# A transformer stack on one core: order of loads, of the first attention, of the norms and of the last sequences, all outside the long loop

## The chip, the cores and the metric

The kernel runs on one core of a Trainium2 chip. The metric is the device time of one execution in microseconds (us). Engines are named as in the profile: PE (TensorE, matmuls), PEld (its weight loads), DVE (VectorE), ACT (ScalarE), POOL (GpSimd), SP (SyncE, which issues the loads and stores).

## The reference

Eight sequences of 256 rows and 128 features pass through one modulated attention, and then through six layers, each a windowed attention with 16 heads of 64 and a gated feed-forward of 341 hidden features. Everything is float32.

```python
x = L0_attn_emb                                            # (8, 256, 128)
mod = (_silu(L0_c) @ L0_wmod).reshape(8, 6, 1, -1)
sa, ca, ga, sb, cb, gb = (mod[:, k] for k in range(6))
ga = (2 * (ga >= 0) - 1) * jnp.maximum(jnp.abs(ga), 0.25)  # gb alike
h = _layernorm(x, axis=-1) * (1 + ca) + sa
x = x + ga * attn(h, W1, W2, W3, Wo)
h = _layernorm(x, axis=-1) * (1 + cb) + sb
x = x + gb * stack(h)

def attn(emb, ...):       # 8 groups of 16 features, softmax over all 256 keys
    q, k, v = (einsum('bse,pe->bsp', emb, W).reshape(B, H, S, D) for W in (W1, W2, W3))
    scores = einsum('bhqd,bhkd->bhqk', _rope(q), _rope(k)) / sqrt(H)
    out = einsum('bhqk,bhkd->bhqd', softmax(scores), v)
    ...                   # and a product with Wo

def stack(x):
    for i in range(6):
        x = attn_layer(shift_tokens(x), ...) + x   # q, k normed and turned by rope, windows of 32, look back by one
        x = ffn_layer(shift_tokens(x), ...) + x    # layernorm, W1, a * gelu(gate), W2
    return x
```

## The kernel before

The program is written engine by engine, each with its own list of instructions in a fixed order; semaphores hold an engine until another has counted far enough. No scheduler moves anything. `CREDIT` (8) is added to many semaphores at the start so that waits of the first passes are already met.

**Start.** SP issues all loads in one row: the constants (`cst`, 640 KB), x (`x1`, 1024 KB, features on the partitions), `cT`, `wmod`, the weights of the first attention, and the first layer's `wqkv`. ACT and DVE form silu of `cT`; PE multiplies it with `wmod` (L527), ACT copies the result to `mod`. Then PE takes the mean over features of each of four chunks of 512 rows (`ln_tensor`, L225) by a product with a constant matrix; DVE subtracts it (L233), ACT squares, PE takes the variance (L228), ACT takes Ln (L247) and Exp (L249) for the inverse root, DVE multiplies (L238) and scales by the modulation (L1249, one instruction for each of eight sequences). POOL sets memory to constants (`memset`) and then splits `wqkv` of the first layer in a high and a low part (`split_weights`, L426: `wqkv_lo` is `wqkv_sb` minus `wqkv_hi`, which ACT has rounded) and forms two rope tables (L417). PE projects V (L542), then Q and K (L551), DVE applies the rope (L1258) and a constant product sums the pairs (L560).

**First attention.** 16 steps `i`, the middle twelve in a loop of two steps a pass. A step holds 8 blocks of 128 queries by 256 keys, in two halves. PE: `a_scores` (L572) of the next step, `a_turn` (L582), which turns a half of P from banks 4 and 5, `a_turn_o` (L603) and `a_attend` (L594), the product with V. DVE: `a_maximum` (L1276, and L1280, the negation), `a_normalise`, `a_stage` (copies of Q and K of the step after next to a fixed place, L1267, L1270), `a_copy_o`. ACT: `a_exps` (L969, 8 a step), `a_copy_p` (L975, two a step: turned P from banks 4 and 5 to `a_pt`, one buffer that lies in `h1`), and `a_stage_v` (L981, V of the next step to a fixed place).

**Second norm.** PE multiplies with Wo for all eight sequences (L632), DVE adds the residual eight times (L1323), then the same norm runs (`ln_tensor`, `ln_vector`, `ln_scalar`) and DVE scales into `h0` (L1333, `modulate`).

**Slots.** 48 slots follow, one for each layer and sequence. In slot `g` two halves of 128 rows go through projection of the next sequence (L671, L674, L675), scores (L724, L731), the product with V (L766), turns in 64-row halves (`turn`, L684), projection out of the sequence before (L788), and the feed-forward of sequence `g` - 3 (`LAG`): up (L806 to L808), gelu, down (L834). Slots 0, 1 and 2 are written out, slots 3 to 46 are a loop on PE and DVE, slot 47 is written out again. SP loads the next layer's weights on the way.

**End.** After slot 47 the feed-forwards of sequences 45, 46 and 47 are left. They use the same banks (7, 1 and 0), so `last_down` does them one after the other; each has two loads of ACT's table, and `final` adds to x. Four stores of 256 KB write the output.

## Time and profile before

| | us |
|---|---|
| three timed runs | 1780.46, 1783.48, 1783.80 |
| the profiled execution | 1771.68 |
| its span, first to last instruction | 1769.9 |
| PE busy in the span | 1633.4 (92%) |
| DVE, ACT, POOL busy | 1340.1, 1292.9, 1061.1 |

The profile is of one execution; its span is what the trace shows, its own time is 1.8 us longer. "Busy" counts the time in which at least one instruction of the engine was under way. The mean granted clock of PE is 0.973 of full speed. In 40 slices of the span, 44 us each, PE is busy 90% or more from the ninth to the last but two, and less in the slices before and behind, where the granted clock is lower too. Row times below are microseconds from the start of the span; in a row's brackets stand the idle time of the engine ahead of it and what ended it.

### The profile page before, as it was taken

Reading aid. Unit: us, or ns where it says so; the run is one execution under the profiler, and the core shown is the slowest. Engines: PE = TensorE matmul, PEld = TensorE weight load, DVE = VectorE, ACT = ScalarE, POOL = GpSimd, SP = SyncE. Lnnn points to the kernel's source line nnn. Section 1 sums busy time; section 2 is a strip of 40 time slices with the busy share of each in tenths; the row PEclk is TensorE's granted clock in tenths of the full one; section 3 lists DMA queues with packets and bytes.
Section 4 is the critical chain, followed back from the end, with each engine's and each line's share of the span. In section 5 each row is a group of like instructions: output and inputs, shape, how many; then the busy total and the mean of one; then the engine's idle time right before and its main releaser. Section 6 shows DMA issues by size and latency. Waiting matters only on the chain.

```text
span 1769.9 us, 88661 instructions
## 1 busy us (share of the span) xinstructions
PE 1633.4 (92%) x36636; PEld 1264.3 (71%) x36636; DVE 1340.1 (76%) x1952; ACT 1292.9 (73%) x2124; POOL 1061.1 (60%) x767
## 2 busy tenths in 40 slices
PE   4898677799999999999999999999999999999985
PEld 2466455677777777777777777777777777777764
DVE  4465666688888878888887888888887878888852
ACT  3687445677877778777788777878777787777763
POOL 4000345567866767867678766668676676767630
PEclk8899889999999999999999999999999999999997
DMA  2000142222242222333222422222422222222220
GB/s 95 1 1 0 25 116 59 52 70 66 67 128 59 67 59 69 103 88 74 53 69 59 128 66 71 69 52 65 122 69 71 66 67 70 70 67 69 66 47 25
DMA packets 75302, 116.88 MB, mean 66 GB/s; under 512 B 17246, under 2 KB 26716, under 8 KB 74332
## 3 DMA queue, kind: packets, MB, share of 16 engines
q1 hardware_dynamic: 75228, 115.99, 26.4%
q8 instruction: 35, 0.57, 0.1%
q14 instruction: 39, 0.32, 0.1%
HBM read 19.04 MB, written 1.05 MB: 11 GB/s over the span
## 4 chain that ended last, share of the span: by engine, by line
PE 87%; issue 6%; ACT 4%; DVE 3%; DMA 0%; POOL 0%; ACTq 0%; SPq 0%; DVEq 0%
PE ps L684 14%; PE ps L788 10%; PE ps L671 9%; PE ps L766 9%; PE ps L731 8%; PE ps L675 7%; PE ps L674 7%; PE ps L834 4%; PE ps L724 2%; PE ps L806 2%; PE ps L808 2%; PE ps L807 2%; PE ps L801 2%; PE ps L795 2%; PE ps L582 1%
## 5 line engine op out<-in xcount | busy, mean ns | idle before, releaser
L411 POOL TENSOR_TENSOR arena<-arena,rnorm 128x1024 f32<-128x1024 f32 x192 | 361.6, 1904 | 352.3 <-ACT rnorm L1030 352.3
L402 POOL TENSOR_TENSOR arena<-arena 128x1024 f32<-128x1024 f32 x192 | 456.6, 2378 | 18.5 <-DVE arena L1349 15.1
L684 PEld LDWEIGHTS ps<-cst,arena 64*128 64x128 f32 x6144 | 224.4, 140 | 127.8 <-issue 119.0
L1345 DVE TENSOR_TENSOR arena<-ps,rope 128x1024 f32<-128x1024 f32 x192 | 234.7, 1222 | 94.9 <-issue 82.1
L684 PE MATMUL ps<-cst,arena 64*128 64x64 f32 x6144 | 276.8, 231 | 17.0 <-ACT arena L1060 9.4
L1066 ACT ACTIVATE arena<-ps 128x512 f32<-128x512 f32 x192 | 114.6, 597 | 175.5 <-PE ps L684 175.2
L1349 DVE TENSOR_TENSOR arena<-ps,rope 128x1024 f32<-128x1024 f32 x192 | 233.2, 1215 | 0.0
L674 PE MATMUL ps<-wqkv_lo,x_hi 128*128 128x512 f32 x576 | 229.2, 398 | 1.1 <-issue 1.1
L675 PE MATMUL ps<-wqkv_hi,x_hi 128*128 128x512 f32 x576 | 230.1, 399 | 0.0
L671 PE MATMUL ps<-wqkv_hi,x_lo 128*128 128x512 f32 x576 | 216.2, 457 | 14.8 <-issue 12.9
L1359 DVE TENSOR_REDUCE norm<-arena 128x16 f32<-128x1024 f32 x192 | 224.3, 1209 | 0.0
L1370 DVE TENSOR_REDUCE rmax<-ps 128x8 f32<-128x512 f32 x192 | 131.8, 686 | 109.0 <-PE ps L731 108.5
L766 PE MATMUL ps<-v_sb,arena 64*32 64x66 f32 x12288 | 166.5, 226 | 35.4 <-issue 19.3
L1019 ACT ACTIVATE arena<-ps 128x1024 f32<-128x1024 f32 x192 | 190.3, 1020 | 11.1 <-DVE arena L1349 11.1
L766 PEld LDWEIGHTS ps<-v_sb,arena 64*32 64x32 f32 x12288 | 138.2, 106 | 73.1 <-issue 62.9
L788 PE MATMUL ps<-arena,wo_sb 128*128 128x256 f32 x768 | 188.5, 389 | 1.2 <-issue 1.2
L731 PE MATMUL ps<-k_t,arena 64*32 64x64 f32 x12288 | 166.6, 224 | 8.2 <-issue 8.2
L1046 ACT ACTIVATE k_t<-ps 128x1024 f32<-128x1024 f32 x96 | 98.4, 1025 | 82.0 <-PE ps L684 79.5
L731 PEld LDWEIGHTS ps<-k_t,arena 64*32 64x32 f32 x12288 | 134.6, 105 | 32.4 <-issue 9.3
L788 PEld LDWEIGHTS ps<-arena,wo_sb 128*128 128x128 f32 x768 | 140.2, 192 | 20.4 <-issue 1.3
L1385 DVE TENSOR_TENSOR arena<-ps,rden 128x512 f32<-128x512 f32 x192 | 132.8, 692 | 14.4
L1374 DVE TENSOR_TENSOR arena<-ps,rmax 128x512 f32<-128x512 f32 x192 | 132.8, 692 | 14.4
(120 smaller groups left out, 2824.2 us busy)
## 6 DMA issues: line engine op xcount, KB each, us to landing
v_sb<-v_nat SPq DMA_DIRECT2D x576, 130.0 KB, 2.4
v_sb<-v_nat SPq DMA_DIRECT2D x192, 65.0 KB, 2.0
wqkv_sb<-wqkv SPq DMA_DIRECT2D x6, 1536.0 KB, 6.8
v_sb<-v_sb SPq DMA_DIRECT2D x96, 65.0 KB, 2.0
wo_sb<-wo SPq DMA_DIRECT2D x6, 512.0 KB, 8.4
w_sb<-w SPq DMA_DIRECT2D x6, 341.0 KB, 7.9
x<-xT SPq DMA_DIRECT2D x1, 1024.0 KB, 6.2
out<-x SPq DMA_DIRECT2D x4, 256.0 KB, 2.3
```

Source lines behind the costliest of these rows:

```text
L402: pool.tensor_tensor(t_cos[:, m, j, :], t_cos[:, m, j, :], t_sin[:, j, :], ALU.add)\
L411: pool.tensor_tensor(x, x, rnorm[:, H * j:H * j + H].unsqueeze(2).to_broadcast([P, H, D]), ALU.mult).then_inc(s[done], 1)
L671: pe.matmul(ps[:, bank + c, :], x_lo[:, m, :], wqkv_hi[:, w], start=True, stop=False)
L674: pe.matmul(ps[:, bank + c, :], x_hi[:, m, :], wqkv_lo[:, w], start=False, stop=False)
L675: mm = pe.matmul(ps[:, bank + c, :], x_hi[:, m, :], wqkv_hi[:, w], start=False, stop=True)
L684: mm = pe.transpose(ps[0:width, bank + t, 64 * c:64 * c + 64], src[r], ident[r, r], tile_position=(64 * t, 0))
L731: mm = pe.matmul(ps[W * w:W * w + W, 4 * g + c, SPAN * hh:SPAN * hh + SPAN], q_t[r, 4 * g + hh, W * w:W * w + W], k_t[r, 4 * g + hh, P * m ...
L766: mm = pe.matmul(ps[W * w:W * w + W, 4 - 2 * g + c, ON * hh:ON * hh + ON], p_t[r, h, W * w:W * w + W], v_sb[r, m, w, VD * h:VD * h + ON], ...
L788: mm = pe.matmul(ps[:, 0, 0:N], wo_sb[:, c, :], o_t[:, c, :], start=(c == 0), stop=(c == H // 2 - 1), skip_group_check=True)
L1345: dve.tensor_tensor(t_cos[:, m, j, :].rearrange("p (h d) -> p h d", h=H), src.rearrange("p a (h d) -> p (a h) d", h=8), tc.unsqueeze(1).to ...
L1349: dve.tensor_tensor(t_sin[:, j, :].rearrange("p (h s d) -> p h s d", h=H, s=2), src.rearrange("p a (h s d) -> p (a h) s d", h=8, s=2)[:, : ...
L1359: dve.tensor_reduce(norm2[:, H * j:H * j + H], sq[:, j, :].rearrange("p (h d) -> p h d", h=H), AX.X, ALU.add).then_inc(s["normed"], 1)
```

## The change

It alters nothing inside the long loop. Part by part:

- **Loads.** `cT` first, then only the 64 KB of the mean matrix, x, `wmod`, and then the rest of the constants in two pieces; two more semaphores tell of them. PE takes the four means before the modulation products, the variances after them; DVE subtracts means first and makes the bf16 copies of the identity and the mask (L1223, L1224) after the scalings.
- **POOL.** It copies V to its fixed place (`a_stage_v`) instead of ACT, and splits the first layer's weights only when the rope is done. The whole memset of `h0` becomes one of eight columns, that of `h1` on DVE too.
- **First attention.** Turned P has two buffers, in `h1` and `h0`; the product with V of step `i` - 1 and the turn of O of step `i` - 2 stand in step `i`, between the two turns. A turn is done in 64-row halves, 16 instructions instead of 8, as in the slots.
- **Second norm.** Product, residual, mean, variance, division and scaling go by chunks of two sequences, with the chunks interleaved on each engine; ACT's first roundings come before the last two chunks' roots.
- **Slots 1 and 2** are a loop of their own on PE and DVE.
- **End.** The last three sequences have banks of their own (`LAST_BANKS`), all up products of one are issued together, those of sequence 45 inside slot 47, and ACT's table loads are shared. The output goes in five stores, the last two of 128 KB.

```diff
+LAST_BANKS = {SLOTS - 3: (7, 6, 1), SLOTS - 2: (4, 5, 2), SLOTS - 1: (7, 6, 1)}
...
-        a_pt = h1[:, 0:2048].rearrange("p (a b c) -> p a b c", a=8, b=2)
+        a_pts = [h[:, 0:2048].rearrange("p (a b c) -> p a b c", a=8, b=2) for h in (h1, h0)]
...
-            sp.dma_start(cst[:, :], consts).then_inc(s["const_loaded"], 16)
+            sp.dma_start(a_cT, cT).then_inc(s["c_loaded"], 16)
+            sp.dma_start(mean_w, consts[:, C_MEAN:C_MEAN + P]).then_inc(s["mean_loaded"], 16)
             sp.dma_start(x1[:, :], xT).then_inc(s["x_loaded"], 16)
-            sp.dma_start(a_cT, cT).then_inc(s["mod_loaded"], 16)
             sp.dma_start(a_wm, wmod).then_inc(s["mod_loaded"], 16)
+            sp.dma_start(ident, consts[:, C_ID:C_ID + P]).then_inc(s["const_loaded"], 16)
+            sp.dma_start(cst[:, C_SUM2:], consts[:, C_SUM2:]).then_inc(s["const_loaded"], 16)
...
+            def a_stage_v(i, k):
+                pool.wait_ge(s["a_pv"], CREDIT + i - 1)
+                pool.tensor_copy(a_vs[:, k, :, :, :].rearrange("p j k d -> p j (k d)"),
+                                 a_v[:, :, bass.ds(i, 1), :, :].rearrange("p j i k d -> p j (i k d)"))\
+                    .then_inc(s["a_v_staged"], 1)
+            pool.wait_ge(s["a_v_ready"], 16)
+            a_stage_v(0, 0)
+            a_stage_v(1, 1)
+            pool.wait_ge(s["a_roped"], 2 * AG)
             for j in range(3):
                 split_weights(0, j)
             table(0, 0)
             table(0, 1)
+            with pool.Fori(1, AH) as two:
+                a_stage_v(pool.snap(2 * two), 0)
+                a_stage_v(pool.snap(2 * two + 1), 1)
             pool.wait_ge(s["a_v_staged"], 2 * AH)
             pool.memset(v_sb[:, :, :, :], 1.0).then_inc(s["zeroed"], 1)
+            pool.wait_ge(s["a_pv"], CREDIT + 2 * AH)
...
-            pe.wait_ge(s["mod_loaded"], 32)
+            pe.wait_ge(s["mean_loaded"], 16)
+            pe.wait_ge(s["x_loaded"], 16)
+            for c in range(NC):
+                ln_mean(pe, c)
+            pe.wait_ge(s["mod_loaded"], 16)
             pe.wait_ge(s["silu_ready"], 1)
             for k in range(6):
                 mm = pe.matmul(ps[:, 7, B * k:B * k + B], a_wm[:, E * k:E * k + E], a_sil, start=True, stop=True)
             mm.then_inc(s["mod_mm"], 1)
-            pe.wait_ge(s["mod_ready"], 1)
-            pe.wait_ge(s["const_loaded"], 16)
-            def x_ready(pe, c):
-                pe.wait_ge(s["x_loaded"], 16)
-            ln_tensor(pe, x1_c, x_ready, 0)
+            for c in range(NC):
+                if c == NC - 1:
+                    pe.wait_ge(s["mod_ready"], 1)
+                ln_var(pe, c, 0)
+            pe.wait_ge(s["const_loaded"], 32)
...
+            def turn(bank, c, src):
+                width = src.shape[1]
+                for t in range(2):
+                    r = slice(64 * t, 64 * t + 64)
+                    mm = pe.transpose(ps[0:width, bank + t, 64 * c:64 * c + 64], src[r], ident[r, r],
+                                      tile_position=(64 * t, 0))
+                return mm
             def a_turn(i, half):
                 pe.wait_ge(s["a_exped"], CREDIT + 8 * i + 4 * half + 4)
                 pe.wait_ge(s["a_pt_ready"], CREDIT + 2 * i + half)
+                pe.sem_inc(s["pe_waited"], 1)
                 for q in range(4):
                     for kh in range(2):
-                        mm = pe.transpose(ps[:, 4 + q // 2, P * (2 * (q % 2) + kh):][:, 0:P],
-                                          a_p[:, 4 * half + q, P * kh:P * kh + P], ident)
+                        mm = turn(4, 2 * q + kh, a_p[:, 4 * half + q, P * kh:P * kh + P])
...
-            def a_step(i, k, before=True, more=True):
-                a_turn(i, 0)
+            def a_step(i, k, turn_before=True, attend_before=True, more=True):
                 if more:
                     a_scores(i + 1, 1 - k, 0)
-                a_turn(i, 1)
+                a_turn(i, 0)
+                if turn_before:
+                    a_turn_o(i - 2)
+                if attend_before:
+                    a_attend(i - 1, 1 - k)
                 if more:
                     a_scores(i + 1, 1 - k, 1)
-                if before:
-                    a_turn_o(i - 1)
-                a_attend(i, k)
+                a_turn(i, 1)
...
+            a_out(0)
+            a_out(1)
+            x1_mean(0)
+            a_out(2)
+            x1_mean(1)
+            ln_var(pe, 0, 1)
+            a_out(3)
+            x1_mean(2)
+            ln_var(pe, 1, 1)
+            x1_mean(3)
+            ln_var(pe, 2, 1)
+            ln_var(pe, 3, 1)
...
+            def last_up(f):
+                a, b, c = LAST_BANKS[f]
+                pe.wait_ge(s["f_split"], CREDIT + f + 1)
+                pe.wait_ge(s["w1_ready"], CREDIT + f + 1)
+                up(ps[:, a, 0:N], 1, 2)
+                up(ps[:, a, N:2 * N], 0, 2).then_inc(s["f_gate_up"], 1)
+                up(ps[:, b, 0:N], 1, 0)
+                up(ps[:, b, N:2 * N], 1, 1).then_inc(s["f_gate_up"], 1)
+                up(ps[:, c, 0:N], 0, 0)
+                up(ps[:, c, N:2 * N], 0, 1).then_inc(s["f_value_up"], 2)
...
+                else:
+                    pe.wait_ge(s["v_copied"], CREDIT + 2 * SLOTS)
+                    pe.wait_ge(s["f_centred"], CREDIT + SLOTS - 1)
+                    last_up(SLOTS - 3)
...
-            slot(1, ff=False)
-            slot(2, ff=False)
+            with pe.Fori(1, LAG) as g:
+                slot(pe.snap(g), ff=False)
             with pe.Fori(LAG, SLOTS - 1) as g:
                 slot(pe.snap(g))
             slot(SLOTS - 1, ahead=False)
...
-            pe.wait_ge(s["f_centred"], CREDIT + SLOTS - 1)
-            mean(SLOTS - 1)
-            variance(SLOTS - 1)
-            for f in range(SLOTS - LAG, SLOTS):
-                last_down(f)
+            down(SLOTS - 3, 7)
+            pe.wait_ge(s["o_normed"], CREDIT + 4 * SLOTS)
+            last_up(SLOTS - 2)
+            mean(SLOTS - 1, 3)
+            last_variance(SLOTS - 1)
+            down(SLOTS - 2, 4)
+            pe.wait_ge(s["f_done"], CREDIT + SLOTS - 2)
+            last_up(SLOTS - 1)
+            down(SLOTS - 1, 7)
...
-            def a_stage_v(i, k):
-                act.wait_ge(s["a_pv"], CREDIT + i - 1)
-                act.activation(a_vs[:, k, :, :, :].rearrange("p j k d -> p j (k d)"),
-                               a_v[:, :, bass.ds(i, 1), :, :].rearrange("p j i k d -> p j (i k d)"), ACT.Copy)\
-                   .then_inc(s["a_v_staged"], 1)
-            def a_step(i, k, more=True):
+            def a_step(i, k):
                 a_exps(i, 0)
+                a_copy_p(i - 1, 1 - k, 1)
                 a_exps(i, 1)
-                a_copy_p(i, 0)
-                if more:
-                    a_stage_v(i + 1, 1 - k)
-                a_copy_p(i, 1)
-            act.wait_ge(s["a_v_ready"], 16)
-            a_stage_v(0, 0)
-            a_step(0, 0)
+                a_copy_p(i, k, 0)
...
+            act.preload_act_table_set("gelu_and_others")
+            gates(SLOTS - 3, 7, 6)
+            round_norm(SLOTS - 2)
             shift(SLOTS - 1)
             square(SLOTS - 1)
-            inverse_deviation(SLOTS - 1)
-            gates(SLOTS - 3)
-            round_norm(SLOTS - 2)
-            gates(SLOTS - 2)
+            act.preload_act_table_set("natural_log_exp_and_others")
+            inverse_deviation(SLOTS - 1, ps[:, 3, N:2 * N])
+            act.preload_act_table_set("gelu_and_others")
+            gates(SLOTS - 2, 4, 5)
             round_norm(SLOTS - 1)
-            gates(SLOTS - 1)
+            gates(SLOTS - 1, 7, 6)
...
+            a_residual(0)
+            a_residual(1)
+            ln_centre(dve, 0, 1)
+            a_residual(2)
+            ln_centre(dve, 1, 1)
+            a_residual(3)
+            ln_centre(dve, 2, 1)
             dve.wait_ge(s["zeroed"], 6)
-            def modulate(b):
-                dve.wait_ge(s["ln_normed"], NC + b // 2 + 1)
-                dve.tensor_scalar(h0[:, HP * b + 1:HP * b + HP], xc[:, N * b:N * b + N], mod[:, 4, b:b + 1],
-                                  mod[:, 3, b:b + 1], ALU.mult, ALU.add).then_inc(s["h0_ready"], 1)
+            modulate(0)
+            ln_centre(dve, 3, 1)
+            for c in range(1, NC):
+                modulate(c)
...
-            dve.memset(h1[:, :], 0.0)
+            dve.memset(h1[:, :].rearrange("p (b t) -> p b t", b=B)[:, :, 0:1], 0.0)
             slot(0, out=False, ff=False)
-            slot(1, ff=False)
-            slot(2, ff=False)
+            with dve.Fori(1, LAG) as g:
+                slot(dve.snap(g), ff=False)
```

How the instructions stand. First PE in the first attention, in the steps behind its loop (L572 and L589 are scores, L582 and L600 turns, L603 and L630 the turn of O, L594 and L621 the product with V). Before:

```order
L582 MATMUL ps<-cst,arena 128x128 x8
L572 MATMUL ps<-f_a 128x256 x4
L582 MATMUL ps<-cst,arena 128x128 x8
L572 MATMUL ps<-f_a 128x256 x4
L603 MATMUL ps<-cst,arena 128x128 x2
L594 MATMUL ps<-h,f_a 32x128 x16
```

and now:

```order
L589 MATMUL ps<-f_a 128x256 x4
L600 MATMUL ps<-cst,arena 128x64 x16
L630 MATMUL ps<-cst,arena 128x128 x2
L621 MATMUL ps<-h,f_a 32x128 x16
L589 MATMUL ps<-f_a 128x256 x4
L600 MATMUL ps<-cst,arena 128x64 x32
```

Scores come ahead of the turn, and the product with V (of the step before) stands between the two halves, where it stood at the end. Second, POOL from its third memset on (L426 and L427 are the splits, L417 and L418 the tables, L488 the copies of V, L490 the memset ahead of the slots). Before:

```order
L382 MEMSET h 128x2056
L383 MEMSET w_hi 128x768
L384 MEMSET w_lo 128x768
L385 MEMSET k_t 128x2304
L426 ISA
L426 TENSOR_TENSOR wqkv_lo<-wqkv_sb,wqkv_hi 128x1024 x3
L417 TENSOR_TENSOR rope<-cst,scl 128x256 x2
L490 MEMSET v_sb 128x4224
```

and now, from behind the memsets:

```order
L488 COPY f_a<-v_sb 128x256 x2
L427 ISA
L427 TENSOR_TENSOR wqkv_lo<-wqkv_sb,wqkv_hi 128x1024 x3
L418 TENSOR_TENSOR rope<-cst,scl 128x256 x2
L500 UNCONDITIONAL_BRANCH
L500 ISA
L488 ISA
L488 COPY f_a<-v_sb 128x256
```

Two copies of V stand ahead of the splits, and a loop with the other fourteen behind the tables. Third, PE in the second half of slot 47 (L834 and L882 are down products, L795 and L828 the mean, L766 and L799 the product with V, L801 and L833 the variance, L684 and L600 turns, L788 and L821 the projection out, L806 to L808 and L843 to L845 up products). Before:

```order
L834 MATMUL ps<-f_a,w_sb 128x256 x3
L684 MATMUL ps<-cst,arena 128x64 x8
L795 MATMUL ps<-f_a,cst 128x256
L766 MATMUL ps<-v_sb,arena 32x66 x64
L801 MATMUL ps<-f_a,cst 128x256
L684 MATMUL ps<-cst,arena 128x64 x16
L788 MATMUL ps<-arena,wo_sb 128x256 x8
L795 MATMUL ps<-f_a,cst 128x256
L801 MATMUL ps<-f_a,cst 128x256
L806 MATMUL ps<-f_hi,w_lo 128x256
```

and now, up to the first up products:

```order
L882 MATMUL ps<-f_a,w_sb 128x256 x3
L600 MATMUL ps<-cst,arena 128x64 x8
L828 MATMUL ps<-f_a,cst 128x256
L799 MATMUL ps<-v_sb,arena 32x66 x64
L843 MATMUL ps<-f_hi,w_lo 128x256
L844 MATMUL ps<-f_lo,w_hi 128x256
L845 MATMUL ps<-f_hi,w_hi 128x256
```

Eighteen up products stand behind the product with V and ahead of the variance, and behind the projection come a down product and the next eighteen where the mean stood.

## Rows read from the trace of the kernel before

**Rows 1.** Busy times by stretch: PE, PEld, DVE, ACT, POOL, PEclk, DMA.

```profile
64.86:178.59 113.73, 97.38 (x1056) 69.91 (x1056) 64.86 (x141) 84.17 (x175) 3.62 (x1) 0.92 0.00 1
178.59:197.09 18.50, 10.71 (x48) 6.56 (x49) 11.60 (x24) 9.49 (x17) 1.03 (x3) 0.90 0.00 0
294.07:331.71 37.64, 29.06 (x717) 22.18 (x713) 23.96 (x32) 20.93 (x35) 22.27 (x16) 0.95 0.24 56
396.33:427.00 30.67, 30.43 (x740) 24.03 (x736) 25.55 (x37) 24.05 (x39) 20.52 (x16) 1.00 0.28 65
331.71:1697.49 1365.78, 1341.40 (x32388) 1057.12 (x32384) 1126.24 (x1584) 1075.75 (x1734) 954.17 (x688) 1.00 0.30 74
1697.49:1769.90 72.41, 46.34 (x764) 37.28 (x760) 20.97 (x44) 31.45 (x49) 9.03 (x10) 0.82 0.10 29
```

**Rows 2.** Timeline of PE at the start: start, length, what.

```profile
13.95 6.41 PE L225 MATMUL ps<-x,cst 128*128 128x512 f32 x8 [0.30 <-ACT mod L931]
20.19 3.60 PE L228 MATMUL ps<-arena,cst 128*128 128x512 f32 x8
```

**Rows 3.** DMA issues from 0 to 20 us: KB, us to landing.

```profile
x<-xT SPq DMA_DIRECT2D x1, 1024.0 KB, 6.2
```

**Rows 4.** Groups of ACT, 0 to 200 us: busy us, mean ns.

```profile
L249 ACT ACTIVATE arena<-arena 128x512 f32<-128x512 f32 x8 | 5.0, 630 | 0.3
...
L247 ACT ACTIVATE arena<-ps 128x512 f32<-128x512 f32 x8 | 4.6, 578 | 0.0
```

**Rows 5.** Groups of DVE, 0 to 200 us.

```profile
L1249 DVE TENSOR_SCALAR arena<-arena,mod 128x256 f32<-128x256 f32 x8 | 9.6, 1265 | 0.0
L1280 DVE TENSOR_SCALAR a_nmax<-a_max 128x4 f32<-128x4 f32 x32 | 8.3, 260 | 3.5
...
L1323 DVE SCALAR_TENSOR_TENSOR x<-ps,gate,x 128x256 f32<-128x256 f32 x8 | 3.5, 480 | 1.3 <-PE ps L632 1.3
...
L1333 DVE TENSOR_SCALAR h<-arena,mod 128x256 f32<-128x256 f32 x8 | 2.7, 408 | 0.0
```

**Rows 6.** Groups of POOL, 0 to 200 us.

```profile
L426 POOL TENSOR_TENSOR wqkv_lo<-wqkv_sb,wqkv_hi 128x1024 fp32r<-128x1024 f32 x3 | 7.2, 2413 | 17.1 <-ACT wqkv_hi L939 17.1
```

**Rows 7.** Timeline of PE in one step of the first attention.

```profile
91.99 1.09 PE L582 MATMUL ps<-cst,arena 128*128 128x128 f32 x8 [0.20 <-ACT arena L969]
93.15 1.13 PE L572 MATMUL ps<-f_a 32*128 32x256 f32 x8
...
97.08 1.08 PE L594 MATMUL ps<-h,f_a 128*32 128x128 f32 x32
98.37 1.09 PE L582 MATMUL ps<-cst,arena 128*128 128x128 f32 x8 [0.21 <-ACT arena L969]
```

**Rows 8.** Timeline of ACT in the same step.

```profile
94.43 0.44 ACT L981 ACTIVATE f_a<-v_sb 128x256 f32 x1
95.75 1.02 ACT L975 ACTIVATE h<-ps 128x1024 f32<-128x1024 f32 x1 [0.88 <-PE ps L582]
96.67 1.56 ACT L969 ACTIVATE arena<-ps,a_nmax 128x256 f32<-128x256 f32 x4
```

**Rows 9.** Timeline of PE at the end of a slot.

```profile
1696.85 0.71 PE L684 MATMUL ps<-cst,arena 64*128 64x64 f32 x16
```

**Rows 10.** Waits of PE in the third slot: total us, times, longest.

```profile
PE ps L766 <- issue: 3.3, 2, 2.5
PE ps L731 <- issue: 2.7, 2, 1.6
...
PE ps L674 <- issue: 1.1, 1, 1.1
```

**Rows 11.** Timeline of PE in the last stretch.

```profile
1731.87 5.89 PE L788 MATMUL ps<-arena,wo_sb 128*128 128x256 f32 x16 [1.16 <-issue]
...
1747.52 2.93 PE L834 MATMUL ps<-f_a,w_sb 128*128 128x256 f32 x6 [1.10 <-DVE f_a L1411]
...
1764.32 1.56 PE L834 MATMUL ps<-f_a,w_sb 128*128 128x256 f32 x6 [1.10 <-DVE f_a L1411]
```

264 lines of the change are left out of this document (139 added, 125 removed).

## The prediction

> **What bounds the kernel now.** I read the stages first [rows 1]: the columns are the stretch, its length, the busy time of PE, PE's weight loads, DVE, ACT and POOL, then the granted clock. The long loop from 331.71 to 1697.49 us is 77% of the span, and PE is busy in 1341.40 of its 1365.78 us; one slot of it is 30.67 us with PE busy 30.43. The change doesn't touch this body. The other 404 us are the five stages around it, and there no engine is full: in the first attention (113.73 us) ACT is busy 84.17 and PE 97.38; in the second norm (18.50 us) DVE leads with 11.60; in a slot ahead of the loop (37.64 us) PE has 29.06; in the last stretch (72.41 us) PE has 46.34 at a mean clock of 0.82. So all the time to be had lies in order and waits. Then I read the timeline of the start and of one attention step, the groups of DVE and ACT, and PE's waits in the third slot. The sum below is against the profiled execution (1771.68 us, of which 1769.9 are span and 1.8 lie outside, unchanged). The median of the three timed runs is 11.8 us above it; I keep that distance and name the result on the median's scale.
>
> **Start, up to the first scores.** Now the first mean product starts at 13.95 us, since it stands behind the modulation products, which wait for a load that is fourth in the queue [rows 2]. In the change it waits for x and a 64 KB slice only. x takes 6.2 us from its issue at 1.2 [rows 3], so it landed at 7.4, behind 640 KB; with almost nothing ahead I put it at 6.2 (bounds 5.5 and 7.4). Four means take 6.4 (8 records at 0.86 apart; at the high level the variances stand 0.43 apart, 3.60 for 8), the six modulation products, which run from 10.95 to 13.65, 2.7: 15.3. First variance 0.9: 16.2. ACT then takes 1.15 us a chunk (Ln 0.578 and Exp 0.630, overlapping a little) [rows 4], four of them: 20.8; division 0.7 and two scalings 0.8: 22.3. Before, PE's next product started at 36.58, so 14.3 are gained. Of these some 7 are one thing: the eight scalings L1249 take 9.6 us, mean 1265 ns, while the same operation and shape as L1333 takes 408 ns each [rows 5]. The difference is POOL's three splits of 2413 ns [rows 6], which lie beside the first and not the second. The change puts the splits behind the rope products, so the scalings run alone. I take -14; with PE at the low level through the variances and x at 7.4 it is -11.5, at best -15.5.
>
> The splits (7.2) and two tables (1.5) now begin when the rope is done, about 8 us ahead of DVE's first staging copies, and end about 1 us past the point where these now start. Cost 0 to 1.1 us, taken as +0.5.
>
> **First attention.** One step takes 6.38 us, from the turn at 91.99 to the one at 98.37 [rows 7]. ACT [rows 8] does eight exponentials (1.56 for four, 3.13 for eight), two copies of turned P (0.92 each, from 95.75 to the next start at 96.67) and the staging of V (0.44, of which 0.35 count), sum 5.3; the rest is the wait for the second turn, which can start only when the first copy has left the two banks (0.88), and a short one for DVE. PE does two turns (1.09, some 1.03 to the next start), two score groups (1.13, 1.06), the turn of O (0.37) and the product with V (1.08, 1.04), sum 5.6. The change takes the staging from ACT (to POOL), gives P a second buffer so that the product with V runs a step late, beside the next scores, and turns in 64-row halves. Sixteen such turns take 0.71 us in the slots [rows 9], 0.65 without the last one's latency, against 1.03 for eight whole ones. So ACT needs 3.13 + 1.84 = 4.97 a step and PE 1.30 + 2.12 + 0.37 + 1.04 = 4.83. I laid the steps on one another: scores of the next step when the first four exponentials end; the maximum (1.24) and its negation reach ACT 2.7 us later, while ACT is in the copy and the second four; the second turn waits for the copy, and ends just as ACT is ready for it. Nothing waits by more than 0.1, and the step comes to 5.0 to 5.2. I take 5.15: the twelve steps at the high clock level give 12 x 1.23 = 14.8. The first two steps run at the low clock level, where the saved PE time is doubled but ACT hides part: 3. The last two and the drain: 2.2. Sum -20. If halves cost on PE what whole ones did, a step is 5.8 and the term -11; at 5.0 it is -22. POOL's memset of V (3.6) delays one DVE negation (L1280 has a mean of 260 ns over 32 [rows 5], from one case of 3.0 us and 31 near 170) now and in the change alike.
>
> **Second norm.** All eight residual additions (L1323, 480 ns each) stand ahead of the first mean, and all eight scalings (L1333) ahead of the first projection [rows 5]. Taken by chunks, three quarters of both leave that path: 2.7 + 2.0 = 4.7. The floor is DVE's 11.60 busy of 18.50 [rows 1], a gain of 6.9. DVE has to end all chunks before the first rope, so I take -6 (bounds -4 and -7). The memset of h1 (1.8) lay beside PE's projections: nothing.
>
> **Slots ahead of the loop.** The third slot has 37.64 us and does less than a loop slot of 30.67. PE waits there for "issue" in 3.3 + 2.7 + 1.1 = 7.1 us [rows 10]; in the second slot the same waits are about 6, and in the loop's later passes (30.43 busy of 30.67 [rows 1]) there is no room for any. What differs is that the slots' code runs for the first time. The change puts slots 1 and 2 in one PE loop, so the second pass meets code that has run. Then it is 30.5 at most and 29 if idle time on other engines shrinks too: -7.5, bounds -1 (the second pass waits 6 as the second slot does) and -10.
> The Trainium skill ("Runtime: NRT & Kernel Launch", section "Instruction fetch mechanics") says that a taken branch out of the fetched window forces a fetch and that kernels prefer full unrolling. By that rule the term would be about 0 and the time 1736. This trace speaks against it for a body of this size: the long loop branches back 43 times, and the pass shown has 0.24 us idle in all.
>
> **End.** The projection of the last sequence takes 5.89 for 16 records at the low level; then three feed-forwards follow one another, since they share banks: their down products start at 1747.5, 1756.5 and 1764.3, and one takes 2.93 at the low level and 1.56 at the high one [rows 11]. In the change the first one's up products lie in the last slot, ahead of a wait, and its gates beside the projection; the second's lie beside the norm of the third. Counted from the end of the projection (1737.4 before), with the durations that the same operations have in this stretch: down of the first 1.5, up of the second 2.1, mean, centring, square and variance 2.2, the uncovered part of a table load 0.6, Ln and Exp 0.8, another load 1.3, the second's gates 1.3, its last products 0.9, down 1.5 and addition 0.6 (the third's rounding and rest lie beside these), its up 2.1, gates and products 1.4, down 1.5, addition and residual 1.1: 18.9, so the last residual ends at 1756 with PE at the high level, and at 1760 at the low one, against 1766.9. The inserted up products push the variance back by 0.9. I take -8 (bounds -5 and -11).
>
> **Sum:** -14 + 0.5 - 20 - 6 - 7.5 - 8 = -55.0; 1771.7 - 55 = 1716.7 by the profiled execution, and 1783.5 - 55 = 1728.5 as a median. All low bounds together give -31, all high ones -66.
>
> **Rivals.**
> 1. The attention step keeps a wait (5.8 us): POOL's copies of V meet DVE's copies, or the halves cost more. For it: both chains are within 0.2 of each other, so any delay shows. Against it: the row of the slots gives 0.65. -46, 1737.
> 2. The short loop gains nothing: its second pass waits for its instructions as the third slot does now, 7.1 us [rows 10]. Against it: the long loop. -47.5, 1736. This is what the rule of "Instruction fetch mechanics" in the Trainium skill comes to.
> 3. PE stays at the high level in the end and x comes early: -64, 1719.
> 4. Slower: the long loop's PE body starts at another address, as less straight code stands ahead of it, and no longer stays at hand from pass to pass. Code run for the first time waits 7.1 us a slot [rows 10]; a third of that in each of the 43 later passes is 102 us against the 55: 1831. It decides from 55/43 = 1.3 us a pass. Against it: a pass of 30.67 with 0.24 idle, and a body that is unchanged.
>
> **How the numbers follow.** Forecast 0.62, rival 1 0.16, rival 2 0.10, rival 3 0.09, rival 4 0.03. The range 1710 to 1748 takes in rivals 1 to 3 and, up to -35, several of their losses together. A measurement tells 0.2% (3.6 us) from no change; all cases but the last are faster by far more: faster 0.96, within 0.2% 0.01, slower 0.03.
>
> **What would show it.** L1249's successor at 0.41 us each and the first V products near 22 us; the step between turns at 5.0 to 5.3; the third slot near 30 us with no issue waits; the last residual 9 us earlier after the projection; the long loop at 30.67 a slot. Wrong would be a step above 5.6, or issue waits in the second pass of the short loop, or any other pace of the long loop.

## The result, and the profile of the changed kernel

| | before | changed |
|---|---|---|
| median of the timed runs | 1781.97 us (4 runs, 1776.37 to 1783.80) | 1716.14 us (4 runs, 1709.83 to 1719.28) |
| profiled execution | 1771.68 us | 1714.45 us |
| its span | 1769.9 us | 1712.6 us |
| mean granted clock of PE | 0.973 | 0.980 |

The ratio is 0.9631, with a 95% interval of 0.9594 to 0.9668: the changed kernel is 3.7% faster. A second series of six runs of it gave 1716.50 us (1713.15 to 1722.66), ratio 0.9659 [0.9631, 0.9687].

The stages first, by windows of the changed kernel's trace: the stretch, its length, the busy time of PE, PEld, DVE, ACT and POOL, the granted clock, the DMA share and GB/s. The first three are the first attention, the second norm, and the projections of sequence 0; then come slots 0, 1, 2 and 3, the slots from 4 to 46, and slot 47 with the end.

```profile
51.44:145.03 93.59, 83.23 (x1313) 60.07 (x1313) 64.48 (x141) 78.99 (x160) 9.39 (x16) 0.91 0.00 1
145.03:159.23 14.20, 12.75 (x48) 8.14 (x49) 8.80 (x18) 6.44 (x13) 1.03 (x3) 0.87 0.00 0
159.23:182.05 22.82, 13.23 (x68) 9.63 (x68) 17.07 (x21) 9.70 (x15) 13.66 (x10) 0.79 0.20 47
182.05:220.55 38.50, 26.51 (x694) 20.26 (x693) 22.80 (x30) 17.01 (x27) 19.56 (x13) 0.81 0.45 122
220.55:254.01 33.46, 28.61 (x714) 22.21 (x713) 23.78 (x32) 20.10 (x33) 19.37 (x13) 0.95 0.27 62
254.01:283.22 29.21, 26.79 (x716) 20.83 (x712) 23.95 (x32) 20.95 (x35) 20.55 (x15) 1.00 0.29 69
283.22:320.27 37.05, 32.59 (x741) 25.53 (x738) 26.53 (x37) 24.28 (x39) 22.38 (x17) 0.95 0.26 62
320.27:1651.06 1330.79, 1309.85 (x31652) 1032.66 (x31649) 1101.11 (x1548) 1051.84 (x1695) 934.16 (x673) 1.00 0.30 74
1651.06:1712.60 61.54, 42.02 (x763) 33.74 (x760) 20.96 (x44) 27.16 (x46) 9.04 (x10) 0.88 0.12 34
```

Here and below, PE is at its high clock level where the granted clock is 1.00, and at its low level where it is 0.5. The attention has lost 20.1 us against [rows 1], and PE and ACT are fuller in it. Slot 2 runs at the high clock level throughout and takes 29.21 us where it took 37.64 [rows 1]. The steady slots are as they were. Cut at the same events in both traces, the time went like this:

| stretch (profiled executions) | before | changed | difference | predicted |
|---|---|---|---|---|
| start to PE's first V product | 36.58 | 22.45 | -14.1 | -14 |
| from there to the first scores | 28.28 | 28.99 | +0.7 | +0.5 |
| first attention, to the first product with Wo | 113.73 | 93.59 | -20.1 | -20 |
| from there to the first rope product on DVE | 21.73 | 17.79 | -3.9 | -6 |
| from there to slot 0 | 19.25 | 19.23 | 0.0 | 0 |
| slots 0 to 3 | 146.06 | 138.22 | -7.8 | -7.5 |
| slots 4 to 46 | 1331.86 | 1330.79 | -1.1 | 0 |
| slot 47 to the end of the last residual | 69.45 | 59.28 | -10.2 | -8 |
| last residual to the end of the span | 2.96 | 2.26 | -0.7 | 0 |
| sum | | | -57.3 | -55 |

**Start.** PE's timeline in the changed kernel (start, length, what, and in brackets the idle time before it):

```profile
6.81 6.37 PE L228 MATMUL ps<-x,cst 128*128 128x512 f32 x8 [6.81 <-DMA x<-xT]
13.02 1.40 PE L547 MATMUL ps<-arena 128*128 128x8 f32 x12
14.28 3.68 PE L232 MATMUL ps<-arena,cst 128*128 128x512 f32 x8
22.45 1.79 PE L559 MATMUL ps<-arena 128*128 128x128 f32 x7 [4.49 <-issue]
```

The mean is first now and its wait is ended by x, 7.1 us earlier than in [rows 2]. The first V product starts 0.1 us behind DVE's last scaling, which ends at 22.34 us. The eight scalings, 9.6 us in [rows 5], take 410 ns each (group of DVE, 0 to 200 us: busy us, mean ns):

```profile
L1299 DVE TENSOR_SCALAR arena<-arena,mod 128x256 f32<-128x256 f32 x8 | 2.9, 410 | 0.1
```

**First attention.** One step of PE, then of ACT, from their timelines:

```profile
98.40 0.71 PE L600 MATMUL ps<-cst,arena 64*128 64x64 f32 x16
99.15 1.13 PE L589 MATMUL ps<-f_a 32*128 32x256 f32 x8
100.41 0.71 PE L600 MATMUL ps<-cst,arena 64*128 64x64 f32 x16
101.05 0.44 PE L630 MATMUL ps<-cst,arena 128*128 128x128 f32 x2
101.42 1.08 PE L621 MATMUL ps<-h,f_a 128*32 128x128 f32 x32
```

```profile
99.24 1.02 ACT L1026 ACTIVATE h<-ps 128x1024 f32<-128x1024 f32 x1
100.16 1.56 ACT L1020 ACTIVATE arena<-ps,a_nmax 128x256 f32<-128x256 f32 x4
101.59 1.04 ACT L1026 ACTIVATE h<-ps 128x1024 f32<-128x1024 f32 x1
```

No row has a bracket, so neither engine has an idle time of 0.15 us or more here. The wait of 0.88 us in [rows 8] is gone. The products with V start 5.00 and 5.09 us apart in turn, 10.1 us for two steps, so the step is 5.05 us where it was 6.37; the recorded texts below, which say 5.08, took one of the longer ones. From 81.98 to 130 us, ACT is busy 46.61 and PE 46.37 of 48.02 us.

**End.** PE's timeline:

```profile
1685.83 3.69 PE L821 MATMUL ps<-arena,wo_sb 128*128 128x256 f32 x16 [1.16 <-issue]
...
1700.23 2.93 PE L882 MATMUL ps<-f_a,w_sb 128*128 128x256 f32 x6 [5.05 <-DVE f_a L1484]
```

The projection runs at the high level in this execution (3.69 us for what took 5.89 in [rows 11]), with the up products of the first feed-forward now ahead of it; it isn't sure to, since in e11_late_loads, with the same code at the end, it took 5.38, and so it did in e1_written, e8_norm_order and e10_all. The down product of the second still comes after 5 us of idle time and at the low level.

### The profile page after: what moved, and what is told of

It reads as the page before. It is cut to its first block, busy times and chain, and to the rows that moved or that the text cites. A ratio compares the mean times of both kernels' runs of the same rounds, so it can differ in the third digit from the quotient of the medians.

```text
span 1712.6 us, 89331 instructions
## 1 busy us (share of the span) xinstructions
PE 1613.6 (94%) x36892; PEld 1250.3 (73%) x36892; DVE 1333.5 (78%) x1952; ACT 1282.2 (75%) x2104; POOL 1066.3 (62%) x783
## 4 chain that ended last, share of the span: by engine, by line
PE 89%; issue 5%; ACT 3%; DVE 2%; DMA 0%; POOL 0%; ACTq 0%; DVEq 0%; SPq 0%
PE ps L600 15%; PE ps L821 10%; PE ps L714 10%; PE ps L799 9%; PE ps L764 9%; PE ps L718 8%; PE ps L717 8%; PE ps L882 4%; PE ps L757 3%; PE ps L843 2%; PE ps L845 2%; PE ps L844 2%; PE ps L833 2%; PE ps L828 2%; PE ps L589 1%
## 5 line engine op out<-in xcount | busy, mean ns | idle before, releaser
L600 PEld LDWEIGHTS ps<-cst,arena 64*128 64x128 f32 x6656 | 243.3, 140 | 148.9 <-issue 140.1
L600 PE MATMUL ps<-cst,arena 64*128 64x64 f32 x6656 | 300.3, 230 | 25.2 <-ACT arena L1101 9.4
L799 PE MATMUL ps<-v_sb,arena 64*32 64x66 f32 x12288 | 165.6, 227 | 26.2 <-issue 10.6
L821 PE MATMUL ps<-arena,wo_sb 128*128 128x256 f32 x768 | 186.7, 386 | 1.2 <-issue 1.2
L799 PEld LDWEIGHTS ps<-v_sb,arena 64*32 64x32 f32 x12288 | 138.1, 106 | 63.4 <-issue 52.0
L821 PEld LDWEIGHTS ps<-arena,wo_sb 128*128 128x128 f32 x768 | 139.0, 190 | 19.8 <-issue 1.3
```

Source lines behind the costliest of these rows:

```text
L600: mm = pe.transpose(ps[0:width, bank + t, 64 * c:64 * c + 64], src[r], ident[r, r], tile_position=(64 * t, 0))
L799: mm = pe.matmul(ps[W * w:W * w + W, 4 - 2 * g + c, ON * hh:ON * hh + ON], p_t[r, h, W * w:W * w + W], v_sb[r, m, w, VD * h:VD * h + ON], ...
L821: mm = pe.matmul(ps[:, 0, 0:N], wo_sb[:, c, :], o_t[:, c, :], start=(c == 0), stop=(c == H // 2 - 1), skip_group_check=True)
```

## The experiments

All are edits of the changed kernel. The table gives the median and range, and the ratio to the kernel before with its interval. The later columns are of the profiled executions: first attention, slots 0 to 3, and the start of slot 47 to the last residual.

| | us | ratio | attention | slots 0-3 | end |
|---|---|---|---|---|---|
| changed, first execution | 1716.14 (1709.83-1719.28) | 0.9631 [0.9594, 0.9668] | 93.6 | 138.2 | 59.3 |
| a1_again | 1716.50 (1713.15-1722.66) | 0.9659 [0.9631, 0.9687] | 93.7 | 135.8 | 61.4 |
| e1_written | 1723.26 (1720.86-1725.61) | 0.9703 [0.9665, 0.9742] | 93.5 | 141.3 | 63.0 |
| e2_two_loops | 1719.01 (1714.24-1722.97) | 0.9673 [0.9629, 0.9717] | 97.1 | 135.2 | 62.6 |
| e3_whole | 1725.35 (1721.97-1731.57) | 0.9722 [0.9680, 0.9765] | 102.3 | 140.2 | 58.3 |
| e4_splits | 1721.39 (1718.75-1723.98) | 0.9693 [0.9654, 0.9732] | 97.2 | 136.3 | 60.6 |
| e5_act_end | 1726.13 (1723.62-1728.66) | 0.9697 [0.9655, 0.9739] | 95.7 | 136.1 | 69.4 |
| e6_pair_body | 2061.01 (2056.10-2070.44) | 1.159 [1.153, 1.165] | 93.5 | 133.6 | 60.8 |
| e8_norm_order | 1716.23 (1711.25-1717.45) | 0.9653 [0.9631, 0.9676] | 93.5 | 128.4 | 61.4 |
| e9_filler | 1711.20 (1709.07-1713.32) | 0.9624 [0.9602, 0.9646] | 89.0 | 140.4 | 60.0 |
| e10_all | 1718.04 (1714.79-1722.24) | 0.9665 [0.9640, 0.9690] | 88.3 | 142.1 | 62.7 |
| e11_late_loads | 1711.11 (1708.06-1716.23) | 0.9612 [0.9566, 0.9657] | 93.5 | 133.1 | 61.1 |
| e12_best | 1706.89 (1704.97-1711.31) | 0.9613 [0.9589, 0.9637] | 88.3 | 135.7 | 58.6 |

**The same kernel again.**

> The changed kernel as it is, once more, to see how far two executions of the same code differ by stage. Theory (the differences of 2 us in slots 0, 1 and 3 and of 3.6 us at the start of the first attention between kernels with equal code there come from the execution: when TensorE's clock rises, and how the first run of the code goes): again differences of 1 to 4 us in these stretches, and slot 2 at 29.2 and the later slots at 30.7 to 0.1 us; time 1712 to 1720. Rival (each build has its own fixed times): all stretches within 0.3 us of the first execution.

Measured: every border of a stage from the first V product to slot 0 is within 0.1 us of the first execution, and slot 2 at 29.21 again. But slot 0 took 38.95 us for 38.50, slot 1 32.45 for 33.46, slot 3 35.19 for 37.05, the end 61.4 for 59.3. The theory holds for the slots and the end, though not here for the attention; e2_two_loops and e4_splits, equal to it in the attention's code, show what may happen there: PE's clock rose one step later, the first step took 8.59 us instead of 5.95, and the attention 3.5 us more. What follows: a stage of one profile is good to 2 to 4 us where code runs for the first time or the clock moves, and to about 0.1 us elsewhere.

**The short loop.**

```
-            with pe.Fori(1, LAG) as g:
-                slot(pe.snap(g), ff=False)
+            slot(1, ff=False)
+            slot(2, ff=False)
```

DVE's loop is written out in the same way.

> The changed kernel with slots 1 and 2 written out again on TensorE and VectorE instead of a loop of two passes. Theory (code that runs for the first time makes TensorE wait, a pass of a loop that has run does not): slot 2 goes from 29.2 back to about 37.6 us, and the first pass of the long loop gets shorter again, from 37.1 to about 34, since it lost 3.1 with the short loop: together +5 us, 1721, with issue waits of 6 to 7 us in slot 2. Rival A (the gain in slot 2 is the order of the other engines, not the code): 0 us, 1716. Rival B (the longer slot 3 has nothing to do with the short loop): +8 us, 1724.

Measured: slot 2 takes 36.16 us instead of 29.21, and PE's timeline there shows the waits (the idle time before each is in the bracket):

```profile
253.15 0.35 PE L764 MATMUL ps<-k_t,arena 64*32 64x64 f32 x16 [1.45 <-issue]
261.67 1.77 PE L799 MATMUL ps<-v_sb,arena 64*32 64x66 f32 x128 [0.74 <-issue]
270.37 0.71 PE L714 MATMUL ps<-wqkv_hi,x_lo 128*128 128x512 f32 x2 [1.48 <-issue]
280.07 0.48 PE L799 MATMUL ps<-v_sb,arena 64*32 64x66 f32 x33 [2.44 <-issue]
```

An issue wait is idle time for which the profile shows no other engine or transfer as the cause; not each is a wait for code, as the 4.49 us at the start show. Those shown, less the one of 0.74 us that the changed kernel has there too, come to 5.4 us, and the granted clock of the slot is 0.95 for 1.00. Slot 3 stays at 37.11, so in this execution its 3.1 us over the kernel before are not the short loop's doing; rival B had that right, rival A is out. By the medians it is +7.1 us, by the profile +3.1 in the slots (slots 0 and 1 were 2 us shorter each this time) and the rest in the end, whose projection ran at the low level. The intervals of the two ratios overlap a little; the slot itself is the evidence. The DMA queue of instructions, q8, tells it directly. In the page of the kernel before and of this one, and then of the changed kernel:

```profile
q8 instruction: 35, 0.57, 0.1%
```

```profile
q8 instruction: 30, 0.49, 0.1%
```

That is 35 and 30 packets, of 16 KB each.

**The first run of a body, alone.**

```
-            with pe.Fori(LAG, SLOTS - 1) as g:
+            with pe.Fori(LAG, 25) as g:
+                slot(pe.snap(g))
+            with pe.Fori(25, SLOTS - 1) as g:
                 slot(pe.snap(g))
```

> The changed kernel with TensorE's long loop cut into two loops of the same body, slots 3 to 24 and slots 25 to 46: the same instructions in the same order, but the second body runs for the first time in slot 25, where all other engines are at their steady pace. Theory (first run of a body costs TensorE issue waits): slot 25 takes 6 to 8 us longer than its neighbours, 1723. Rival (the waits of the slots ahead of the loop come from the other engines starting up): slot 25 like its neighbours, 0 us, 1716.

Measured, by windows of slots 24, 25 and 26:

```profile
939.30:969.95 30.65, 30.39 (x738) 23.99 (x736) 25.38 (x36) 24.06 (x39) 20.45 (x15) 1.00 0.52 149
969.95:1003.44 33.49, 30.87 (x741) 24.22 (x737) 25.54 (x37) 24.28 (x39) 20.69 (x16) 1.00 0.27 62
1003.44:1034.10 30.66, 30.43 (x741) 24.03 (x737) 25.39 (x36) 24.74 (x40) 20.55 (x15) 1.00 0.28 66
```

The first run costs 2.8 us, where 6 to 8 were expected, and happens once, with two issue waits of 1.2 us; q8 has 6 packets more than the changed kernel. So the mechanism is shown, and its price isn't fixed: 2.8 us behind a loop with 2.4 us of issue waits and the clock at 1.00, and 7.0 us in slot 2 behind two slots of straight code, with 5.4 us of them and the clock at 0.95. Why more packets come late there stays open.

**What stays at hand.**

```
-            with pe.Fori(LAG, SLOTS - 1) as g:
-                slot(pe.snap(g))
+            with pe.Fori(1, (SLOTS - 1 - LAG) // 2 + 1) as two:
+                slot(pe.snap(2 * two + 1))
+                slot(pe.snap(2 * two + 2))
```

> The changed kernel with two slots written out in the body of TensorE's long loop, 22 passes of about 2 x 1500 instructions instead of 44 of 1500. The instructions and their order are the same. Theory A (what stays at hand is far more than one slot's code): slot 4 costs its first run like slot 3, +3 to +5 us, all later slots 30.7, 1720. Theory B (one slot's code, 6 packets of 16 KB in the instruction queue, is about all that stays, so that each pass is fetched again): packets in the instruction queue through the whole loop and 3 to 7 us of waits a slot, +130 to +300 us, 1850 to 2000.

Measured: theory B, and above its range: +345 us where 130 to 300 were expected. Slots 4 to 46 take 1675.10 us instead of 1330.8, 8.0 us a slot. PE's waits between 1000 and 1074 us (total, times, longest), then the queues in the same window:

```profile
PE ps L764 <- issue: 6.3, 4, 1.8
PE ps L757 <- issue: 3.0, 1, 3.0
PE ps L600 <- issue: 1.7, 2, 1.0
```

```profile
q1 hardware_dynamic: 2496, 4.00, 22.7%
q8 instruction: 12, 0.20, 1.1%
```

Each of the 22 passes fetches 12 or 13 packets again, 309 in all for the kernel, and the 3.0 us wait is at the head of the body, behind the jump back. The issue waits make 11.0 us in these 74; the rest is clock (0.93 granted there) and what waits behind. In the changed kernel q8 moves nothing between 352 and 1653 us. The window from 500 to 600 us:

```profile
q1 hardware_dynamic: 4563, 6.42, 27.0%
q14 instruction: 5, 0.04, 0.1%
```

The Trainium skill ("Runtime: NRT & Kernel Launch", section "Instruction fetch mechanics") gives PE room for 2048 instructions, filled in blocks of 16 KB. The traces agree with both: a body of some 1500 instructions (736 products and 736 weight loads a slot) stays, one of 3000 doesn't. Its remark that kernels prefer full unrolling where possible doesn't hold here for a body that fits; e1_written shows it.

**Loads ahead of the instructions.**

```
             def layer_body(layer, more):
                 first = snap(sp, layer * B)
-                if more:
+                late = isinstance(layer, int) and layer == 0
+                if more and not late:
                     load_qkv(layer + 1)
-                load_up(layer)
-                load_out(layer)
+                if not late:
+                    load_up(layer)
+                    load_out(layer)
...
+                if late:
+                    load_qkv(layer + 1)      # behind two_steps of sequence 3
...
             load_qkv(0)
+            load_up(0)
+            load_out(0)
             sp.wait_ge(s["zeroed"], 6)
```

> The changed kernel with three loads of SyncE moved: the weights of layer 1's q, k and v (1.5 MB) are asked for three sequences later, and those of layer 0's output and feed-forward (0.85 MB) ahead of the first sequence instead of in slot 0. Theory (TensorE's wait of 6.1 to 6.7 us in slot 0 is for a packet of instructions that stands behind these 2.4 MB): that wait shrinks to 1 to 2 us, slot 0 from 38.5 to 33 or 34 us, 1711. Rival (the wait is the price of code that runs for the first time, whatever else is on the DMA): slot 0 as it was, 0 us, 1716.

PE's longest issue wait among the slots is in slot 0; this is its row in the timeline of the changed kernel:

```profile
198.01 0.67 PE L799 MATMUL ps<-v_sb,arena 64*32 64x66 f32 x26 [6.13 <-issue]
```

The queues in 184 to 191 us (no instruction packet, 76.9% of all DMA engines' time taken), and the same wait in e11_late_loads:

```profile
q1 hardware_dynamic: 603, 1.26, 76.9%
```

```profile
194.01 0.67 PE L805 MATMUL ps<-v_sb,arena 64*32 64x66 f32 x26 [2.29 <-issue]
```

Measured: the wait falls by 3.8 us, slot 0 to 35.12. By the medians it is -5.0 against the changed kernel, but the intervals of the ratios overlap; the wait itself is the evidence. The packet of instructions that comes just before the wait ends moves at 195.6 us in the changed kernel and at 191.2 us here. The theory holds, though 2.3 us of wait stay where 1 to 2 were expected: more than half of it was a packet of instructions behind 2.4 MB of weights that nobody needed yet. The wait isn't new: slot 0 of the kernel before has one of 6.08 us at the product with V.

**Whole turns.**

```
-                        mm = turn(4, 2 * q + kh, a_p[:, 4 * half + q, P * kh:P * kh + P])
+                        mm = pe.transpose(ps[:, 4 + kh, P * q:P * q + P],
+                                          a_p[:, 4 * half + q, P * kh:P * kh + P], ident)
```

The copy on ACT reads the turned P in the new order.

> The changed kernel with P of the first attention turned by whole 128 x 128 blocks (8 a half step) instead of 64-row halves on two row tiles (16). Theory (the step is now bound by TensorE and ScalarE together, PE being busy 4.8 of 5.08 us): 2 x 0.38 us more of PE a step, step 5.5 to 5.8 us, 16 steps, +7 to +11 us, 1723 to 1727. Rival (ScalarE alone sets the step; the turns lie under its exponentials): step 5.1 to 5.2, +1 us, 1717.

```profile
94.31 1.06 PE L610 MATMUL ps<-cst,arena 128*128 128x128 f32 x8 [0.22 <-ACT h L1027]
...
99.89 1.06 PE L610 MATMUL ps<-cst,arena 128*128 128x128 f32 x8
```

Measured: the step is 5.62 us (5.58 and 5.66 in turn), +0.57; the attention +8.7. The theory holds: with whole turns PE sets the step, and ACT waits 0.7 to 0.8 us for the turns.

**Splits first.**

```
+            for j in range(3):
+                split_weights(0, j)
             pool.wait_ge(s["a_v_ready"], 16)
             a_stage_v(0, 0)
             a_stage_v(1, 1)
-            pool.wait_ge(s["a_roped"], 2 * AG)
-            for j in range(3):
-                split_weights(0, j)
             table(0, 0)
```

> The changed kernel with GpSimd's three weight splits and two tables ahead of the first attention's staging again, free to start as soon as ScalarE has rounded the weights, as before the change. Theory of the prediction (moving the splits is what made VectorE's eight scalings short, 7 us): +6 to +7 us, 1722. Rival (the scalings by chunks end beside ScalarE's first rounding, so that only the last pair meets a split, and the move of the splits is worth little by itself): +0 to +1.7 us in the scalings and -0.7 us in the staging copies, 1715 to 1717.

DVE and POOL in that kernel, by their timelines:

```profile
20.68 4.67 DVE L1298 TENSOR_SCALAR arena<-arena,mod 128x256 f32<-128x256 f32 x2
25.27 2.37 DVE L1301 CAST ident_bf<-cst 128x128 bf16<-128x128 f32 x1
27.56 0.41 DVE L1302 CAST mask_bf<-cst 128x512 bf16<-128x512 f32 x1
```

```profile
20.29 7.27 POOL L427 TENSOR_TENSOR wqkv_lo<-wqkv_sb,wqkv_hi 128x1024 fp32r<-128x1024 f32 x3 [11.69 <-ACT wqkv_hi L989]
```

Measured: between the two. The last two scalings took 4.67 us instead of 0.73, +3.9; the staging copies took 0.65 less; and 3.5 us are one more step of the attention at the low level, which e2_two_loops had too, without this edit. So the median of 1721.39 us may meet the theory's 1722 by luck in part. Three instructions of DVE, each as long as one split: DVE doesn't run slower beside POOL, it waits once for each whole instruction. That is how the Trainium skill has it too ("SBUF — State Buffer", section "Terms": the port pair is held for the full instruction and the loser blocks), and the 9.6 us of [rows 5] were three scalings of 2.4 and five of 0.4 to 0.8.

**V on ACT, and the old end.** `a_stage_v` is taken from POOL, and the end has the order and the banks of before:

```
                 a_exps(i, 1)
                 a_copy_p(i, k, 0)
+                if stage:
+                    a_stage_v(i + 1, 1 - k)
...
-                    last_up(SLOTS - 3)
...
-            down(SLOTS - 3, 7)
-            last_up(SLOTS - 2)
-            mean(SLOTS - 1, 3)
...
+            mean(SLOTS - 1)
+            variance(SLOTS - 1)
+            for f in range(SLOTS - LAG, SLOTS):
...
+                gates_up(f)
+                pe.wait_ge(s["f_done"], CREDIT + f)
+                values_up(f)
+                down(f)
```

> The changed kernel with two parts undone that lie in different stages, each read from its own stage of the trace. First attention: the staging of V is on ScalarE again (one 128 x 256 copy a step). Theory (ScalarE is full, 4.97 of the 5.08 us of a step): step 5.35 to 5.45 us, +5 us; rival (TensorE sets the step, the copy finds room): 5.08 to 5.15. End: the last three feed-forwards share banks 7, 1 and 0 and follow one another behind the last norm, as before the change. Theory: from the start of the last projection to the last residual 33 to 35 us instead of 24.5, +9 to +10 us; rival (the gain came from the clock, not from the banks): +4 us or less. Together 1726 to 1731.

ACT over one step of e5_act_end, by its timeline:

```profile
99.02 0.42 ACT L1019 ACTIVATE f_a<-v_sb 128x256 f32 x1
99.44 1.57 ACT L1007 ACTIVATE arena<-ps,a_nmax 128x256 f32<-128x256 f32 x4
100.89 1.04 ACT L1013 ACTIVATE h<-ps 128x1024 f32<-128x1024 f32 x1
101.79 1.60 ACT L1007 ACTIVATE arena<-ps,a_nmax 128x256 f32<-128x256 f32 x4
```

Measured: the step is 5.31 us (5.25 and 5.37 in turn), +0.26, where 5.35 to 5.45 was expected: ACT's rows touch one another but for 0.07 us, so it is now the engine that sets the step. The stage is only 2.1 us longer where 5 were expected, in part because the last products with V ran at the high level in this execution (1.08 us for 1.62). From the start of the last projection to the last residual it takes 34.7 us; before the change it was 35.1, in the changed kernel 24.5 and 24.9. Of these 10 us, 2 lie in the projection, which ran at the low level here (5.64 us for 3.69), and 8.2 behind it (29.0 us for 20.8). Against e1_written, e2_two_loops and e11_late_loads, whose projection was at the low level too (25.8 to 26.2 us), it is 8.5 to 8.9. The theory holds in the main: the banks, together with the order and the table loads that go with them, are worth 8 to 9 us; the edit doesn't take the three apart.

**Another order of the second norm** (ACT, PE, DVE).

```
-            ln_square(act, 3, 1)
...
             high(0, 0)
+            ln_inverse(act, 2, 1)
+            ln_square(act, 3, 1)
             high(0, 1)
-            ln_inverse(act, 2, 1)
...
-            copy_v(0, 0)
...
             inverse_norms(0, 0)
+            copy_v(0, 0)
...
-            v(0, 0)
...
             q(0, 1)
+            v(0, 0)
...
+            rope_products(0, 0, 0)
+            modulate(3)
```

> The changed kernel with another order in the second norm and in the projections of sequence 0: ScalarE rounds x and inverts the third deviation ahead of the last square, and computes the inverse norms ahead of the copy of V; VectorE takes the first rope product ahead of the last modulation; TensorE projects the second q ahead of the first v. Theory (VectorE's 1.8 us wait for ScalarE, TensorE's 6.3 us before the first v and GpSimd's 3.7 us before the first scaling are order alone): slot 0 starts 4 to 6 us earlier, 1711. Rival (GpSimd's chain of rotations and scalings, 14 us, sets the start of slot 0, or slot 0 waits longer for its code by what it starts earlier): 0 to -2 us, 1715.

Measured: no change of the time, and for neither theory's reason. Counted from the first product with Wo, the first rope product came 0.7 us later and slot 0 4.9 us later. Slots 0 to 3 took 128.4 us, 7 to 10 us less, 7 of them in slot 0 (31.65 us). In the product with V there, where the changed kernel waits 6.13 us, PE has no such wait now (128 products in 2.09 us). A packet of instructions moved at 190.4 us, ahead of the densest stretch of DMA (194 to 200 us). The order was a loss that the fetch paid back.

**Products that nobody reads.**

```
+            def fill(n, out):
+                for _ in range(n):
+                    pe.matmul(out, ident, cst[:, 0:N], start=True, stop=True)
...
             last_variance(SLOTS - 1)
+            fill(8, ps[:, 0, 0:N])
             down(SLOTS - 2, 4)
```

> The changed kernel with 21 products added on TensorE whose results nobody reads, put where it has nothing to do: 3 before and 5 after the first scores, 5 in the drain of the first attention, 8 in the last stretch while the last norm is computed. Theory (what these stretches lose is TensorE's low clock level after an idle time: 59 to 67 us at 0.5, the out-products at 0.5, the down product of 2.93 us instead of 1.5): -3 us at the start of the attention, -2 us in its drain and the first products with Wo, -3 us in the last stretch, 1709. Rival (the clock doesn't follow from a few products, or the products come in the way): 0 to +3 us, 1718.

The windows from the first scores to the first product with V, and from the last projection to the last residual, in e9_filler and then in the changed kernel:

```profile
51.30:61.81 10.51, 8.77 (x100) 6.53 (x99) 6.91 (x14) 7.37 (x18) 0.00 (x0) 1.00 0.01 2
...
1684.67:1706.84 22.17, 17.11 (x90) 14.23 (x90) 7.54 (x17) 10.12 (x19) 2.77 (x5) 1.00 0.05 18
```

```profile
51.44:64.94 13.50, 10.41 (x88) 7.28 (x88) 7.34 (x14) 8.00 (x18) 0.00 (x0) 0.57 0.01 2
...
1685.83:1710.34 24.51, 16.00 (x74) 13.16 (x74) 7.54 (x17) 10.12 (x19) 2.76 (x5) 0.86 0.05 17
```

Measured: the theory's places and sizes, -3.0, -1.4 (products with Wo to the first rope product 16.36 us for 17.79), -1.6 in the rest of the attention, -2.3 in the end; the down product takes 1.56 us. Slot 0 starts 6.4 us earlier, and slots 0 to 3 give 2 to 5 of that back. The time is 5 us less, and only two of the six executions of a1_again lie below the slowest of these six, though the intervals of the ratios overlap. The range is 4.2 us, for 9.5 in a1_again.

**Together.** The memset of V in pieces, beside the edits shown:

```
-            pool.memset(v_sb[:, :, :, :], 1.0).then_inc(s["zeroed"], 1)
+            for u in range(U):
+                for w in range(4):
+                    ms = pool.memset(v_sb[:, u, w, :], 1.0)
+            ms.then_inc(s["zeroed"], 1)
```

> Both sets of edits, the other order in the second norm and the added products, and GpSimd's memset of V (3.6 us) in eight pieces, since VectorE's 128 x 4 negation beside it waited for the whole instruction (1.95 us, ScalarE 1.66 us behind it). Theory: the sum of the two and -1.5 us, 1702 to 1706. Rival (the stages hide each other's gains): 1711 or more.

> The changed kernel with what the earlier runs showed to pay: the three loads of SyncE moved as in e11_late_loads (slot 0 shorter by 3.4 to 3.8 us there), the 21 added products of e9_filler (first attention to the first rope product -6.1 us, last projection to last residual -2.3 to -2.7), and GpSimd's memset of V in eight pieces (-0.7 in the drain). Theory: the gains lie in different stages and add up to 12 us, 1704. Rival (as in e9_filler, where slots 0 to 3 took 140.4 us in place of 135.8 to 138.2: the earlier start is lost again to waits for instructions in slots 0 to 3, which fall at other places since the added instructions shift the code): 1709 or more.

Measured: e10_all is the rival: slot 0 starts 3.3 us earlier, and that is lost in slots 0 to 3 (142.1 us). Without the order of e8 and with the loads moved, e12_best takes 1706.89 us, halfway between its theory (1704) and its rival (1709). That is 9.6 less than a1_again, and its five runs lie between 1704.97 and 1711.31, where ten of the changed kernel lie between 1709.83 and 1722.66; but the two were not timed side by side, and by the ratios 0.9613 stands to 0.9631 and 0.9659, with intervals that overlap. By the ratios it is also no better than e11_late_loads (0.9612), so how much the whole gains is not settled. By stages it kept 5.3 us in the attention, 1.4 in the norm and 0.7 to 2.8 in the end, but only 0 to 2.5 in slots 0 to 3: slot 3 has a new wait.

```profile
289.38 0.43 PE L819 MATMUL ps<-v_sb,arena 64*32 64x66 f32 x2 [3.06 <-issue]
```

The 3.1 us are in the first run of the long loop's body, where the changed kernel waits 2.1 at most. That the added instructions moved the borders of the packets would explain it; no run shows it.

## Why the prediction was right

The forecast was 1728 us with a range of 1710 to 1748; the time is 1716. By its own steps:

1. **The distance between profile and median (wrong in size).** The sum said -55.0 from one profiled execution to the next, and it was -57.2 (1771.68 to 1714.45), 1716.7 forecast for 1714.5. The 11.8 us by which the median of before stood above its profile were carried over as a constant. But that profile was one execution at the fast end of a spread (of the executions of the kernel before that were timed beside the experiments, the fastest took 1771.06 us, and their medians lie from 1777.66 to 1783.54), while the changed kernel's first profile is only 1.7 us below its median. This step holds 10 of the 12 us by which the forecast missed.
2. **Start, -14: right (-14.1), its reason half right.** The mean at 6.81 was put at 6.2; the modulation products took 1.4 us for 2.7, as the clock had risen ahead of them; and behind the variances DVE, with 1.37 us a chunk, sets the pace and not ACT with 1.15, which costs another 0.7. The three errors cancel, which is luck. The 7 us of the scalings were put down to the move of the splits. e4_splits gives that move 3.9 of them; the order by chunks has the first six scalings done before ScalarE has rounded any weights, and the other 3 are left to it.
3. **Splits beside the staging, +0.5: right (+0.7).** The copies L1322 and L1325 took 0.42 and 0.81 us beside POOL's tables, for 0.28.
4. **First attention, -20: right (-20.1).** The step is 5.05 us for 5.15 forecast. Of the 1.32 us, e3_whole gives 0.57 to the half turns (the prediction put whole turns at a step of 5.8 and -11; with them it is 5.62, and the stage -11.4) and e5_act_end 0.26 to V on POOL. If these add, the other 0.5 is what the second buffer and the order bring, which no run took apart. The start of the stage still depends on the clock, by 3.5 us.
5. **Second norm, -6 (bounds -4 and -7): wrong in size, -3.9.** Two things were not counted: the products with Wo ran at the low level (in e3_whole, e4_splits and e9_filler, where PE was at the high one, the stretch is 16.36 us, -5.4), and DVE waits 1.80 us for an inversion that stands behind a square and the roundings on ACT. That wait is real, but e8_norm_order, which took it out, has DVE wait 3.52 us for PE's projection ahead of the first rope product in its place.
6. **Slots ahead of the loop, -7.5: right in its mechanism, its sum in part by luck (-7.8, and -10.3 in the second execution).** The prediction had all of it in slot 2. Slot 2 gave 8.4 us; slots 0 and 1 gave 2.6 that nobody forecast, and slot 3 took 3.1 back. Slot 2 took 29.2 to 29.3 us in all executions with the short loop, and in the first had no issue wait above 0.74. That it is the code that was missing, e1_written, e2_two_loops, e6_pair_body and the packets of q8 show together. Slot 3 was not foreseen to take 1.3 to 3.1 us more than before; e1_written clears the short loop of it, and the cause stays open. Slot 0's wait was not looked at before the change; e11_late_loads shows that more than half of it is the 2.4 MB of weights.
7. **End, -8: right (-10.2).** Counted from the end of the last projection, as the prediction did, it is -8.4 (29.2 to 20.8 us); the projection at the high level brought 2.2 more in this execution, and slot 47 ahead of it is 0.4 longer. e5_act_end gives the whole stage back (34.7 us for 35.1, and 29.0 for 29.2 behind the projection).
8. **Long loop, 0: right.** 30.67 us a slot but for those in which weights change, in both kernels; rival 4 needed 1.3 us a pass.

Of the rivals, 1 needed a step of 5.8 us, and 2 issue waits in the second pass of the short loop, which is slot 2; neither came. Rival 3 came in part: PE is at the high level in the projection, but not in the second down product, and x didn't come early.

## What to carry to other kernels

Straight code that runs once costs PE a wait at some of its 16 KB blocks; a loop whose body stays at hand (1500 instructions here) pays once, and one whose body doesn't (3000) pays in every pass, 8 us a slot. So count the instructions of a loop's body before unrolling it, and keep bulk loads that nobody needs yet away from stretches of new code. And where the trace shows PE idle and then at its low level in dense work on the path, a few products that nobody reads can be worth more than a better order. Check each such stage by its granted clock, since a single execution doesn't tell a gain of 3 us from the spread.

## What the runs showed of the chip that was not expected

- PE's code comes over the DMA engines in packets of 16 KB that can be counted by queue: 30 in the changed kernel, 35 with the two slots written out, 36 with a second copy of the body, 309 with a body of two slots. In the changed kernel none moved between 184 and 191 us, while weights took 76.9% of the engines' time.
- DVE beside POOL waits once for each whole POOL instruction: 2.4 us for a 128 x 1024 split, 1.95 us for what was left of a memset of 3.62. In eight pieces that start 0.5 us apart (e10_all, e12_best) the same memset delays no negation by more than 0.14 us: the group of the negations has a mean of 197 ns at the end of e12_best's attention, 424 in the changed kernel's.
- After idle times of 2.1 and 3.1 us with 1.3 us of work between them PE was at its low level (0.57 granted from 51.44 to 64.94 us); with eight added products in them it was at 1.00 (e9_filler, 51.30 to 61.81 us).
- The same instructions in the same stage can take 3.5 us more in one execution than in the next, by when PE's clock rises. The added products don't make the time steady by themselves: six executions of e9_filler spread over 4.2 us, but six of e10_all over 7.5 and five of e12_best over 6.3, with the same products in them.
